# Mean layers of a four-layer graph network: weights applied ahead of the mean, transposed counts resident in SBUF, column moments from turned tiles

## What is computed

```
agg = segment_sum(x[src], dst) / max(deg, 1)              # the mean over neighbours
L1:  o = agg @ W_l + b_l + x @ W_r                        # then batch norm over the nodes (column mean
     o = leaky((o - o.mean(0)) * rsqrt(o.var(0) + eps) * gamma + beta) + x     # and variance), leaky relu
L2:  o = x @ W1.T + b1 + agg @ W2.T + b2
L3:  o = where(deg > 0, x @ W1 + b1 + (x - agg) @ W2 + b2, x)
after each layer:  x = layernorm(x + o)
```

## Time and profile before

| | |
|---|---|
| median of 3 runs | 1466.75 us (1466.03 to 1467.74) |
| profiled execution, own time | 1468.84 us |
| its span | 1467.2 us |
| busy in the span | PE 1278.2, DVE 1032.9, ACT 895.6, POOL 742.7 us |
| instructions | 20151 |

### The profile page before, as it was taken

The page is one execution under the profiler, slowest core; times in us unless marked ns, Lnnn a source line. Parts: engine busy times, 40 slices in busy tenths (PEclk is TensorE's granted clock), DMA queues, the critical chain, the costliest instruction groups (busy, mean ns, idle before and its releaser), DMA issues. The chain is left out here.

```text
span 1467.2 us, 20151 instructions
## 1 busy us (share of the span) xinstructions
PE 1278.2 (87%) x5987; PEld 1020.4 (70%) x5987; DVE 1032.9 (70%) x1769; ACT 895.6 (61%) x818; POOL 742.7 (51%) x527
## 2 busy tenths in 40 slices
PE   3947999999999999999999933997989838895997
PEld 2835778887887788878877722785668616784886
DVE  3223899999999999999999942447833577244434
ACT  1116999999999999999999821445530135133112
POOL 0037788888888888888888110007611134133000
PEclk9977999999999999999999966998999969998999
DMA  5767777877777777777777126762033101421321
GB/s 191 277 214 173 151 154 152 162 152 148 153 154 152 156 160 161 152 149 153 154 153 138 19 27 202 265 242 93 36 115 113 54 22 50 144 90 51 119 100 49
DMA packets 107392, 198.09 MB, mean 135 GB/s; under 512 B 34434, under 2 KB 39728, under 8 KB 107336
## 3 DMA queue, kind: packets, MB, share of 16 engines
q0 software_dynamic: 71120, 108.28, 37.5%
q1 hardware_dynamic: 33728, 84.24, 16.8%
q10 hardware_dynamic: 2488, 4.89, 1.0%
HBM read 152.21 MB, written 37.11 MB: 129 GB/s over the span
## 5 line engine op out<-in xcount | busy, mean ns | idle before, releaser
L481 POOL DMA_INDIRECT G<-q_dram,idx_all x168 | 342.6, 2039 | 55.0 <-issue 44.9
L760 PE MATMUL ps_x<-w_hi,hT_hi 128*128 128x512 f32 x672 | 269.0, 400 | 1.3 <-DVE hT_lo L559 1.3
L760 PE MATMUL ps_x<-w_lo,hT_hi 128*128 128x512 f32 x672 | 262.4, 391 | 0.0
L760 PE MATMUL ps_x<-w_hi,hT_lo 128*128 128x512 f32 x672 | 261.6, 389 | 0.0
L473 POOL DMA_INDIRECT G<-p_dram,idx_all x168 | 174.8, 1040 | 146.2 <-issue 143.3
L760 PEld LDWEIGHTS ps_x<-w_hi,hT_hi 128*128 128x128 f32 x672 | 126.2, 188 | 31.6 <-issue 1.7
L760 PEld LDWEIGHTS ps_x<-w_hi,hT_lo 128*128 128x128 f32 x672 | 126.2, 188 | 27.3
L760 PEld LDWEIGHTS ps_x<-w_lo,hT_hi 128*128 128x128 f32 x672 | 126.2, 188 | 25.2
L1322 ACT CAST n_T_hi<-n_ps_T 128x512 fp32r<-128x512 f32 x40 | 22.5, 589 | 190.4 <-PE n_ps_T L1596 190.4
L1584 PE MATMUL n_ps_m<-X_hi,adjT 128*128 128x512 f32 x300 | 120.8, 403 | 19.8 <-issue 19.8
L799 PE MATMUL n_ps_out<-w_hi_n,n_T_hi 128*128 128x512 f32 x300 | 126.3, 421 | 13.0 <-DVE n_T_lo L1556 5.1
(11 more groups left out here) (244 smaller groups left out, 2872.6 us busy)
## 6 DMA issues: line engine op xcount, KB each, us to landing
adjT<-adjT_dram SPq DMA_DIRECT2D x30, 640.0 KB, 4.0
ea_raw<-in_eaT SPq DMA_DIRECT2D x84, 128.0 KB, 4.3
adj_dram<-adj_sb POOLq DMA_DIRECT2D x42, 210.2 KB, 4.6
adj_dram<-zeros SPq DMA_DIRECT2D x11, 640.5 KB, 4.3
adj_in<-adj_dram SPq DMA_DIRECT2D x10, 640.0 KB, 4.6
adjT_dram<-adjT_sb SPq DMA_DIRECT2D x10, 640.0 KB, 5.8
w_raw_n<-in_w POOLq DMA_DIRECT2D x5, 1024.0 KB, 7.1
n_xs<-X SPq DMA_DIRECT2D x20, 256.0 KB, 2.3
```

The source lines that it names most:

```text
L481: g.indirect_dma_start(G[:, b.slot, c * D:(c + 1) * D], None, q_dram, bass.IndirectOffsetOnAxis(ap=idx_all[:, i:i + 1], axis=0), compute_o ...
L760: last = t.matmul(ps_x2[c % 2][:, :], h[:, b.slot, e], w[:, k, :], start=(k == 0 and i == 0), stop=(k == KD - 1 and i == 2))
```

## The change

`mean_layer` is replaced by one function `graph_layers`, one block for layers 1 to 3, with all tile loops written out.

- **Order of the product and the mean.** Instead of `mean(x) @ W` the kernel computes `U = x @ W` for all tiles first, splits U into `U_hi` and `U_lo`, and sums U over the neighbours: 12 matmuls for U, 20 for the sum, as before, but the division is folded into the evacuation. In layer 3 the own weights become W1 + W2.
- **Look-ahead in layer 0.** It now makes `x @ W_l` (U of layer 1) instead of `x @ W_r`. ACT writes `U_hi`, and DVE writes `U_lo` at the end of a later step; the single bank `ps_n` is free only after both. `X_hi` (ACT) and `X_lo` (POOL) are gone.
- **Layer 1** has per tile sums (20), turning x (4), own product (12), and turning the finished Y (`turned_own`, 4 more). DVE takes `bn_stats` of the turned tile: four instructions of 128 columns. At the end four `bn_aggr`, small 128x4 arithmetic, two diagonal tiles and two fp32 matmuls with ones spread scale and shift.
- **Layer 2** turns x and does both products (24 matmuls) per tile while the batch norm is applied, then all sums; **layer 3** the same with all products first, then all sums. X is turned from where it lies, without a DMA.
- **Resident counts.** `adjT_rest` holds tiles 2 to 9, loaded once in layer 1; 20 of the 30 loads of 640 KB go.
- **Moved work.** The final `(y - mean) * rs` is a DVE `tensor_scalar` in place of an ACT activation. The low part of one weight matrix is a POOL `tensor_tensor` 128x2048, after layer 1's last product. SP clears 27 preparation semaphores before its first load of the edge phase.

```diff
# first_layer, ACT step2
-                        for t in (X[:, cols(b.number())], X_hi[:, cols(b.number())]):
-                            a.activation(t, y_out[:, b.slot, :], ACT.Identity, scale=rs[1][:, :], bias=nmr[:, :]).then_inc(x_new, 1)
+                        a.activation(X[:, cols(b.number())], y_out[:, b.slot, :], ACT.Identity, scale=rs[1][:, :], bias=nmr[:, :]).then_inc(x_new, 1)
...
-                        a.copy(Z[:, cols(n.number())], ps_n).then_inc(z_ready, 1)
+                        a.copy(U_hi[:, cols(n.number())], ps_n).then_inc(z_ready, 1)
# first_layer, POOL step2
-                    b = s.at(-3)
-                    if b.real():
-                        wait(x_new, b.count(2))
-                        g.tensor_tensor(X_lo[:, cols(b.number())], X[:, cols(b.number())], X_hi[:, cols(b.number())].bitcast(F32),
-                                        ALU.subtract).then_inc(xlo_ready, 1)
# first_layer, DVE step2, at the end of the step
+                    low = s.at(-6)
+                    if low.real():
+                        dve_.wait_ge(z_ready, low.count(1) + R)
+                        v.tensor_tensor(U_lo[:, cols(low.number())], ps_n, U_hi[:, cols(low.number())].bitcast(F32), ALU.subtract).then_inc(xlo_ready, 1)
# first_layer, PE step2, before the product into ps_n
-                        pe.wait_ge(z_ready, n.count(1) + R - 1)
+                        if n.at(-1).real():
+                            pe.wait_ge(xlo_ready, n.at(-1).count(1))
# edge_phase, SP
+                for s in sems_to_clear:
+                    sp.sem_clear(s)
# graph_layers, SP
+                for r in range(2, R):
+                    sp.dma_start(adjT_rest[:, r - 2, :], adjT_dram[r * P:(r + 1) * P, :]).then_inc(a_in[r - 2], 16)
# graph_layers, POOL
+                wait(split_hi, 3)
+                g.tensor_tensor(slot_w(w_lo, 1), slot_w(w_raw, 1), slot_w(w_hi, 1).bitcast(F32), ALU.subtract).then_inc(split_lo, 1)
+                wait(sh_ready, 1)
+                for r in range(R):
+                    if r >= 2:
+                        wait(y_ready, r - 1)
+                    wait(tsc_ready, r + 1)
+                    g.tensor_tensor(t_be[:, r % 2, :], tmp[:, r % 2, :], shift[:, :], ALU.add).then_inc(tbe_ready, 1)
...
# graph_layers, ACT, while the batch norm is applied
+                for s in range(R + 3):
+                    if 2 <= s <= R + 1:
+                        u_high(2, s - 2)
+                    if 1 <= s <= R:
+                        high(2, s - 1)
+                    if s < R:
+                        deviation(s)
+                    if s >= 3:
+                        own_kept(s - 3)
# graph_layers, DVE, layer 1 and the batch norm
+                for r in range(R):
+                    if r + 1 < R:
+                        low(1, r + 1)
+                    dve_.wait_ge(r_out, r + 1)
+                    v.tensor_tensor(Y[:, cols(r)], ps_b[0][:, :], vec[0][:, :], ALU.add).then_inc(ya_ready, 1)
...
+                    v.scalar_tensor_tensor(Y[:, cols(r)], ps_m[r % 2][:, :], rdeg[:, r:r + 1], Y[:, cols(r)], ALU.mult, ALU.add).then_inc(yb_ready, 1)
...
+                    if r >= 1:
+                        column_stats(r - 1)
+                v.tensor_tensor(vec[1][:, :], vec[1][:, :], vec[2][:, :], ALU.add).then_inc(v_sum, 1)
+                column_stats(R - 1)
...
+                for k in range(KD):
+                    dve_.sem_inc(turn, 1)
+                    v.bn_aggr(mv_c[:, k, :], st_c[:, k, :]).then_inc(agg_c, 1)
...
+                for s in range(R + 3):
+                    if s + 1 < R:
+                        scaled(s + 1)
+                    if s < R:
...
+                        v.scalar_tensor_tensor(t_be[:, s % 2, :], t_be[:, s % 2, :], 0.01, t_be[:, s % 2, :], ALU.mult, ALU.max).then_inc(act_ready, 1)
+                    if 1 <= s <= R:
+                        reciprocal(s - 1)
+                    if s < R:
...
+                        v.scalar_tensor_tensor(y[:, s % 2, :], X[:, cols(s)], 2.0, t_be[:, s % 2, :], ALU.mult, ALU.add).then_inc(y_ready, 1)
+                    if 1 <= s <= R:
+                        result(s - 1)
+                    if s < R:
+                        stats(s)
+                    if 2 <= s <= R + 1:
+                        u_low(2, s - 2)
+                    if s < R:
+                        aggregate(s)
+                    if 1 <= s <= R:
+                        low(2, s - 1)
# graph_layers, PE
+                turned(1, 0)
+                for r in range(R):
+                    sums(1, r)
+                    if r + 1 < R:
+                        turned(1, r + 1)
+                    own_product(1, r)
+                    if r >= 1:
+                        turned_own(r - 1)
+                turned_own(R - 1)
...
+                for i, ready in ((0, dg_ready), (1, sh_dg_ready)):
+                    pe.wait_ge(ready, KD)
+                    t.matmul(ps_m[i][:, :], ones[:, :], tmp[:, i, :], start=True, stop=True).then_inc(sc_out, 1)
+                turned(2, 0)
+                for r in range(R):
+                    u_product(2, r)
+                    if r + 1 < R:
+                        turned(2, r + 1)
+                    own_product(2, r)
+                for r in range(R):
+                    sums(2, r)
+                    if r == R - 2:
+                        turned(3, 0)
+                for r in range(R):
+                    if r + 1 < R:
+                        turned(3, r + 1)
+                    u_product(3, r)
+                    own_product(3, r)
+                for r in range(R):
+                    sums(3, r)
```

More of the change, by code:

```diff
@@ new lines, in high, with u_high, deviation @@
+                def high(layer, r):
+                    n = no(layer, r)
+                    if n >= 2:
+                        act.wait_ge(r_out, n - 1)
+                    act.wait_ge(T_ready, n + 1)
+                    a.copy(xT_hi[:, n % 2, :], ps_T[n % 2][:, :]).then_inc(xhi_ready, 1)
+                def u_high(layer, r):
+                    act.wait_ge(u_out, un(layer, r) + 1)
+                    a.copy(U_hi[:, cols(r)], ps_a[r % 2][:, :]).then_inc(uhi_ready, 1)
+                def deviation(n):
+                    act.wait_ge(mv_ready, n + 1)
+                    a.activation(sd[:, n % 2:n % 2 + 1], mv[:, n % 2, 1:2], ACT.Sqrt, bias=eps_col[:, :]).then_inc(sd_ready, 1)
@@ new lines, in _ @@
+                for r in range(R):
+                    deviation(no(2, r))
+                    if r == 1:
+                        act.wait_ge(raw_in0, 32)
+                        weights(0)
+                    if r == 4:
+                        act.wait_ge(wsum, 1)
+                        weights(1)
+                act.wait_ge(keep_ready, 1)
+                for s in range(R + 1):
+                    if s < R:
+                        high(3, s)
+                    if s >= 1:
+                        u_high(3, s - 1)
@@ L1360, in _ @@
+                for s in range(R + 1):
+                    if s < R:
+                        if s >= 2:
+                            act.wait_ge(y_ready, no(3, s - 2) + 1)
+                        a.activation(tmp[:, s % 2, :], X[:, cols(s)], ACT.Identity, scale=keep[:, s:s + 1]).then_inc(xk_ready, 1)
+                    if s >= 1:
+                        deviation(no(3, s - 1))
             @block.gpsimd
@@ new lines, in reciprocal, with result, column_stats @@
+                def reciprocal(n):
+                    dve_.wait_ge(sd_ready, n + 1)
+                    v.reciprocal(rs[:, n % 2:n % 2 + 1], sd[:, n % 2:n % 2 + 1]).then_inc(rs_ready, 1)
+                def result(n):
+                    r = n % R
+                    dve_.wait_ge(rs_ready, n + 1)
+                    v.tensor_scalar(X[:, cols(r)], y[:, n % 2, :], mv[:, n % 2, 0:1], rs[:, n % 2:n % 2 + 1],
+                                    ALU.subtract, ALU.mult).then_inc(x_new, 1)
+                def column_stats(r):
+                    n = P if r < R - 1 else LASTR
+                    dve_.wait_ge(yT_ready, r + 1)
+                    for k in range(KD):
+                        last = v.bn_stats(st_c[:, k, r * 6:(r + 1) * 6], ps_yT[r % 2][:, k * P:k * P + n])
+                    last.then_inc(yst_ready, 1)
@@ new lines, in _ @@
+                low(3, 0)
+                for s in range(R):
+                    if s + 1 < R:
+                        low(3, s + 1)
+                    u_low(3, s)
+                    dve_.wait_ge(r_out, no(3, s) + 1)
+                    if s == 0:
+                        dve_.wait_ge(v_sum, 2)
+                    v.tensor_tensor(Y[:, cols(s)], ps_b[s % 2][:, :], vec[0][:, :], ALU.add).then_inc(ya_ready, 1)
+                for s in range(R + 1):
+                    if s == 0:
+                        dve_.wait_ge(ya_ready, 2 * R)
+                    sums_of(3, s, with_kept)
@@ L1582, in sums_in @@
+                def sums_in(n, r, dt):
                     for k in range(R):
```

(4 more changed lines are left out.)

654 lines of the change are left out of this document (263 added, 391 removed).

## The result

The changed kernel takes 1435.7 us (median of four runs, 1430.12 to 1436.64) against 1466.39 us of the kernel before beside it. The ratio is 0.978, with a 95% interval of 0.9763 to 0.9796: 31 us faster. The profiled execution has a span of 1435.0 us and an own time of 1436.64. The forecast was 1428, in a range of 1410 to 1448.

What follows compares the result with a forecast made beforehand. Between layers 1 and 3 PE often stood still, so most gain must be stalls. From 1084, terms of 343.4 us gave end 1427.4; less 0.45 is 1427, rounded to 1428 for the restart behind layer 0; range 1410 to 1448.

Steps and rivals of the forecast that it cites:

- as summed: Likeliest case for the whole kernel: the time follows the summed stage estimates, 1418 to 1440 us; chance 0.55.
- lengthening to the first sum: Layer 0: later look-ahead products and a cooler PE clock make it 12 us longer, bounds 4 and 16.
- layer 1: Layer 1's stage: 78 us today plus eight `turned_own` of 0.44 us gives 81 us, with DVE's work covered by PE.
- batch norm to the first turn: From layer 1's last product to the first turn of a new X: 22 us, 15 fewer than 37.
- applied, with products: Batch norm applied while layer 2's products run: 64 us, 11 more than 53, but holding ten more products.
- way to layer 3: Between layer 2's sums and layer 3's products: `low(3, 0)` stands behind the last tile's whole norm, about 5 us.
- the ring through one bank: Layer 0: each product into `ps_n` waits for ACT's `U_hi` and DVE's `U_lo`; 11.2 us, plus 1 for the clock.
- POOL's `X_lo` and ACT's `X_hi` in layer 0 give nothing else back: Layer 0: dropping these two instructions was claimed to save nothing beyond what the sum had already counted.
- The collision: Batch norm: DVE's vector sum is held while POOL subtracts 128x2048; 3.8 us taken, bounds 0.8 and 4.4.
- PE is the bound: Applied batch norm: per tile PE needs 5.9 us against DVE's 5.3, so PE sets the time with 0.6 to spare.
- The rival in which DVE and PE interlock: Applied batch norm: their waits interlock, a tile takes 7 us, +11 us and clock +5, 1439 to 1448 us; chance 0.18.
- The slower rival: Jumps over the fp32 variant stall PE in each of 30 sums; at 2.1 us each, 1491 us; chance 0.03.

## Why the prediction was right, step by step

The likeliest case, "as summed" (1418 to 1440), is what happened. The span of 1435.0 us is 7.6 over the sum's 1427.4; 0.6 of that is the first sum of the kernel before, at 1084.57 where the sum starts from 1084. The rest is spread:

| step | forecast | measured |
|---|---|---|
| lengthening to the first sum | 12 | 14.5 |
| layer 1 | 81 | 82.1 |
| batch norm to the first turn | 22 | 24.3 |
| applied, with products | 64 | 64.9 |
| layer 2's sums | 46 | 46.6 |
| way to layer 3 | 5 | 4.8 |
| layer 3, products and sums | 61 + 45.4 | 60.7 + 45.5 |
| end | 7 | 7.1 |

- **Layer 0: the size was right because two errors cancelled.** The stage grew by 12.7 us; the rest to 14.5 is the restart (3.2 in place of 2.1) and the edge part (0.8). But the ring through one bank cost 18.9 us (103.73 against 84.80), where 11.2 plus 1 were worked out. 12.7 of them are idle time, against the 11.2: the pattern of the waits was right. 6.2 are busy time, against the 1 that I had added for the clock; three products ran partly at 1.2 GHz and took 5 us more together. And the sentence "POOL's `X_lo` and ACT's `X_hi` in layer 0 give nothing else back" is wrong: the stage got back 4.9 us (84.80 against 89.67, both with two banks), 2.3 to 3.1 with POOL's instruction; another 1.4 is what two banks are worth to the kernel before. That the two errors nearly cancelled (18.9 - 6.3 = 12.6) was luck.
- **Batch norm: the mechanism was right, terms of it too small.** The collision came where it was forecast and cost 4.2 (4.83 less 0.6) where I took 3.8. By the Trainium skill (SBUF — State Buffer, Terms) DVE and GpSimd hold their shared port pair exclusively for a whole instruction; the trace agrees, with 4.83 us beside a POOL instruction of 4.49 and 1.59 beside pieces of 1.34. The two fp32 matmuls took 3.75 us, not 2.3: the earlier trace rows ran at a granted clock of 1.00, and these two, behind 9 us of idle PE, at 0.50. Four `bn_aggr` of 60 values took 1.28, not 1.0. That is 2.2 us. From the end of POOL's first add to the first turn it took 6.9 us where 5.7 were worked out: the leaky relu was stretched to 1.73 us while POOL added for the second tile. Smaller terms, above all the copy and the scaling (0.9 in place of 1.4), gave 0.8 back.
- **Applied batch norm: PE is the bound**, as forecast: busy 61.81 of 62.27 us, with one wait of 0.5 for `X`. The rival in which DVE and PE interlock found its moment once and no more: the result of one tile was held by POOL from 0.54 to 1.50 us.

```profile
1248.22 1.50 DVE L1405 TENSOR_SCALAR X<-y_n,mv_n,rs_n 128x512 f32<-128x512 f32 x1
```

- **The slower rival** (a stall of PE in each of the 30 sums) did not come. By the page Runtime: NRT & Kernel Launch of the Trainium skill (Instruction fetch mechanics) a taken branch to an unloaded target stalls; the waits of PE behind 1270 us hold one entry without a releaser, of 0.3 us, and whether a target was unloaded here no trace shows:

```profile
PE ps_u L794 <- DVE xT_lo_n L1377: 4.4, 1, 4.4
PE ps_sum L1571 <- issue: 0.3, 1, 0.3
```

- **Where the gain came from.** 33.3 of the gained 51 us lie between the first turn and layer 3's first product. The windows of that stretch, before and after, and what PE waited for in it before (the 21.9 include 18.1 that belong to the batch norm):

```profile
1198.77:1348.40 149.63, 121.42 (x520) 96.46 (x520) 82.28 (x146) 51.20 (x88) 51.77 (x38) 0.89 0.23 78
1205.47:1321.76 116.29, 109.65 (x489) 89.54 (x489) 81.84 (x145) 25.93 (x53) 24.40 (x17) 0.95 0.02 6
```

```profile
PE n_ps_T L1636 <- DMA n_xs<-X: 21.9, 3, 18.1
PE n_ps_m L1584 <- issue: 17.7, 2, 13.7
PE n_ps_out L799 <- DVE n_T_lo L1556: 5.1, 5, 1.7
PE n_ps_out L799 <- DVE n_T_lo L1434: 1.6, 1, 1.6
```

PE stood still for 28.2 us there and now does for 6.6: the two restarts (17.7), the wait for the copied X (3.8) and the per-tile waits (6.7) are gone, and waits of 1.5, 0.5 and 4.4 us are left. Its own work is 11.8 us shorter; 36 fewer transposes of 0.11 us make 4 of that, the rest goes with a granted clock of 0.95 in place of 0.89. No run takes the new order alone away, nor the single block, nor the turning without a DMA, so how the 33.3 us divide among these parts of the change is not shown. The batch norm gave 12.2, layer 3, with fewer transposes, 5.2, the end 0.4. Layer 0 and layer 1 took 19 back.

## What to carry to other kernels

When a consumer is split over two engines, count the buffers that it frees: an added second reader of a single bank cost some 18 us here, and a second bank, for which there was room, took it back. Keep long POOL instructions out of chains in which DVE works with two operands in SBUF; give the work to DVE in a wait that is there, or cut it in pieces. And read a transfer's removal by what waited for it: 20 loads fewer were worth nothing, where one split done 4 us earlier gave 7.

## What the runs showed of the hardware

- A DVE operation of 128x4 values is held like a large one: 1.42 us, to within 0.01 us of the end of POOL's instruction, where alone it takes 0.16. A `tensor_scalar` with one tile from SBUF was held to 1.50 (alone 0.54).
- A stall can make the next work dearer, and not alike in each execution: behind waits of 4.66, 2.82, 2.81 and 2.60 us PE's matmuls went to 0.43 us apart in three products and stayed at 0.23 in the third; the same program run again (waits of 4.62, 2.82, 2.62 and 2.60) had them at 0.43 behind all four. Without the waits the same 321 matmuls took 6.2 us less of busy time.
- `bn_stats` of 128 columns takes 0.88 us for four in a row, and `bn_aggr` of 60 values 1.28 for four. Two fp32 matmuls 128x128 by 128x512 took 3.75 us at the lower clock.
